# A transformer block pair on one Trainium2 core: the first attention loop one tile deeper

## What is computed

```
y = causal depthwise conv(x, 32 taps per sequence) + b
h = rmsnorm(y);  q = h q_w.T (16 heads of 128);  k, v = h k_w.T, h v_w.T (4 heads of 128)
q, k = rope(rmsnorm(q)), rope(rmsnorm(k))
hidden = y + softmax(causal(q k.T / sqrt(128))) v  @ o_w.T
x = x + hidden + moe(rmsnorm(hidden))           # 8 experts, top 2          -> layer 0
x = x + lora(adaLN transformer block(x, cond))  # attention, gelu FFN, top 1 of 8 -> layer 1
```

## Time and profile before

| | us |
|---|---|
| median of 3 runs | 723.17 |
| lowest, highest | 722.83, 726.57 |
| span of the profiled execution, first to last instruction | 724.2 |
| PE busy | 636.6 (88%) |
| DVE busy | 445.5 (62%) |
| ACT busy | 323.2 (45%) |
| POOL busy | 256.2 (35%) |

### The profile page before, as it was taken

One profiled execution on the slowest core, in us unless ns is written; L12 is line 12 of the kernel. 1 busy time (PEld: TensorE's weight loads), 2 busy tenths in 40 slices (PEclk: granted clock), 3 DMA queues, 4 the chain that ended last, 5 costly groups with the idle time before them and its releaser, 6 DMA issues.

```text
span 724.2 us, 12467 instructions
## 1 busy us (share of the span) xinstructions
PE 636.6 (88%) x4932; PEld 514.3 (71%) x4932; DVE 445.5 (62%) x804; ACT 323.2 (45%) x830; POOL 256.2 (35%) x257
## 2 busy tenths in 40 slices
PE   5379888889999688799995999999999998779997
PEld 2168657568777566688874888888888876558786
DVE  6999998767797766476548346236236235862363
ACT  5155455454567313343423555445444443346440
POOL 6619999914542403163214224014012003432100
PEclk9778999989999888899996999999999999879999
DMA  7500000000000005644510012001000002010013
GB/s 302 222 4 1 2 1 2 0 2 1 1 3 1 1 3 184 173 132 143 159 60 1 0 60 63 26 30 60 1 1 2 1 1 60 0 31 29 1 47 129
DMA packets 12361, 35.15 MB, mean 49 GB/s; under 512 B 2040, under 2 KB 3576, under 8 KB 11792
## 3 DMA queue, kind: packets, MB, share of 16 engines
q1 hardware_dynamic: 12304, 34.36, 14.3%
HBM read 33.24 MB, written 1.11 MB: 47 GB/s over the span
## 4 chain that ended last, share of the span: by engine, by line
PE 64%; POOL 14%; DVE 11%; ACT 5%; issue 3%; DMA 1%; SPq 0%; DVEq 0%; POOLq 0%; ACTq 0%
PE ps L1284 16%; PE ps L1285 15%; PE ps L1286 15%; PE ps L1377 5%; DVE yT L884 4%; POOL hid L479 4%; PE ps L1532 4%; POOL yT L481 3%; PE ps L1357 3%; POOL nrt L503 2%; PE ps L1683 2%; ACT work L645 1%; PE ps L1520 1%; ACT junk L580 1%; DVE strm_lo L1153 1%
## 5 line engine op out<-in xcount | busy, mean ns | idle before, releaser
L1153 DVE SCALAR_TENSOR_TENSOR strm_lo<-ps,col,strm_hi 128x512 fp32r<-128x512 f32 x32 | 24.0, 751 | 114.3 <-ACT strm_hi L763 113.2
L448 POOL TENSOR_TENSOR w_lo<-raw_w,w_hi 128x1024 fp32r<-128x1024 f32 x22 | 54.5, 2497 | 111.2 <-ACT w_hi L588 111.2
L1284 PE MATMUL ps<-act_hi,w_hi 128*128 128x512 f32 x160 | 65.4, 409 | 5.6 <-POOL act_lo L535 3.3
L747 ACT ACTIVATE work<-ps,col 128x512 f32<-128x512 f32 x64 | 44.2, 690 | 51.2 <-PE ps L1286 51.1
L1284 PE MATMUL ps<-w_hi,act_hi 128*128 128x512 f32 x160 | 65.1, 407 | 0.6 <-ACT junk L580 0.6
L1285 PE MATMUL ps<-act_lo,w_hi 128*128 128x512 f32 x160 | 64.1, 401 | 0.0
L1286 PE MATMUL ps<-act_hi,w_lo 128*128 128x512 f32 x160 | 64.1, 400 | 0.0
L1285 PE MATMUL ps<-w_lo,act_hi 128*128 128x512 f32 x160 | 63.9, 399 | 0.0
L1286 PE MATMUL ps<-w_hi,act_lo 128*128 128x512 f32 x160 | 63.5, 397 | 0.0
L1377 PE MATMUL ps<-raw_w,raw_s 128*128 128x256 f32 x256 | 58.8, 388 | 1.9 <-ACT raw_s L653 1.9
L1377 PEld LDWEIGHTS ps<-raw_w,raw_s 128*128 128x128 f32 x256 | 49.8, 195 | 12.7 <-issue 3.8
(11 more groups left out here) (179 smaller groups left out, 1569.7 us busy)
## 6 DMA issues: line engine op xcount, KB each, us to landing
raw_w<-in_w_attn SPq DMA_DIRECT2D x16, 512.0 KB, 4.7
raw_s<-in_w_moe SPq DMA_DIRECT2D x11, 384.0 KB, 4.4
raw_w<-in_w_qkv SPq DMA_DIRECT2D x6, 512.0 KB, 6.1
work<-comb_dram SPq DMA_DIRECT2D x10, 256.0 KB, 3.8
work<-comb_dram SPq DMA_DIRECT2D x18, 128.0 KB, 2.8
raw_w<-in_w_o SPq DMA_DIRECT2D x1, 2048.0 KB, 8.4
raw_s<-in_w_ffn SPq DMA_DIRECT2D x8, 256.0 KB, 2.7
bd<-in_w_ada SPq DMA_DIRECT2D x1, 1536.0 KB, 10.8
```

The lines of the kernel that those rows point to most:

```text
L448: G.tensor_tensor(flat(w_lo[:, slot]), raw_p[:, raw_slot, :], flat(f32(w_hi[:, slot])), ALU.subtract).then_inc(s_piece_lo, 1)
L747: A(dst[:, h * BANK:(h + 1) * BANK], src, ACT.Identity, bias=c_(b, 4 * j + h)).then_inc(s_q1_copied, 1)
L1153: V.scalar_tensor_tensor(flat(strm_lo[:, n % SS]), ps[:, 4 + n % 2, :], c_("bv", 4 * (u // CHUNKS) + h), flat(f32(strm_hi[:, n % SS])), AL ...
L1284: mm(dst, ah, bh, start=start and i == 0, stop=False, **flags)
```

## The change

The loops on TensorE, ScalarE and VectorE get a tenth step, and the back of the chain is one tile further behind. Step s is now: on TensorE the first two banks of `proj(s)`, `pv0(s-2)`, the other four banks, `oproj(s-2)`, `turn_qk(s)`, `scores0(s)`, `turn_y(s+1)`; on VectorE `rope(s)`, the head of softmax s-1, the addition of tile s-2, the tail of softmax s-1; on ScalarE the copies of two banks, the four copies of the value products of s-2, the other banks, three copies of qkT, exp of s-1, two copies of qkT, `take_y`. The factors, taps and DMAs keep their places on POOL and SP. The waits on bank 7 and the sums of squares of hid move by one step, and the transposes of hn of the first three tiles stand inside `oproj(7)` after four heads, those of the next three after twelve.

```diff
@@ -636,10 +636,10 @@
                 for h in range(4):
                     square(src[:, h * DH:(h + 1) * DH], DH, ssq[:, t % 2, at + h:at + h + 1])
 
-            def take_qkT(t):
+            def take_qkT(t, ks):
                 if t >= 1:
                     act.wait_ge(s_s0, t)
-                for k in range(QK):
+                for k in ks:
                     f = QK * t + k
                     act.wait_ge(s_qkT_in_psum, f + 1)
                     A(qkT[:, k * BANK:(k + 1) * BANK], ps[:, QK_BANK[k], :], ACT.Copy).then_inc(s_qkT_copied, 1)
@@ -654,28 +654,29 @@
 
             act.wait_ge(s_y1, DK)
             take_y(0)
-            for s in range(TILES + 1):
+            def exp0(t):
+                act.wait_ge(s_s0_shifted, t + 1)
+                A(sm_e[:], sm_s[:], ACT.Exp).then_inc(s_e0, 1)
+
+            for s in range(TILES + 2):
                 if s < TILES:
                     take_proj(s, 0)
-                if s >= 1:
-                    act.wait_ge(s_s0_shifted, s)
-                    A(sm_e[:], sm_s[:], ACT.Exp).then_inc(s_e0, 1)
+                    take_proj(s, 1)
+                if s >= 2:
+                    take_pv0(s - 2, range(HKV))
                 if s < TILES:
-                    for k in range(1, QK):
+                    for k in range(2, NPROJ):
                         take_proj(s, k)
-                if s >= 1:
-                    take_pv0(s - 1, (0, 1))
+                    take_qkT(s, range(3))
+                if 1 <= s <= TILES:
+                    exp0(s - 1)
                 if s < TILES:
-                    take_proj(s, QK)
-                if s >= 1:
-                    take_pv0(s - 1, (2, 3))
-                if s < TILES:
-                    take_qkT(s)
+                    take_qkT(s, range(3, QK))
                 if s < TILES - 1:
                     take_y(s + 1)
 
-                if s >= TILES - 1:
-                    for t in range(TILES - 1) if s == TILES - 1 else (TILES - 1,):
+                if s >= TILES:
+                    for t in range(TILES - 1) if s == TILES else (TILES - 1,):
                         act.wait_ge(s_hid_attn, t + 1)
                         square(hid[:, t, :], D, stat[:, 16 + t:17 + t])
             moe_slice_hi(0)
@@ -979,17 +980,23 @@
                 link(V.tensor_copy(act_hi[:, :, s], h2[:, :, s]))
                 V.tensor_tensor(act_lo[:, :, s], h2[:, :, s], f32(act_hi[:, :, s]), ALU.subtract).then_inc(s_h2_ready, 1)
 
-            for s in range(TILES + 1):
-                if s >= 1:
+            def add_attn(t):
+                dve.wait_ge(s_o0, t + 1)
+                dve.wait_ge(s_squares, (4 * QK + 1) * t + 1)
+                V.tensor_tensor(hid[:, t, :], ps[:, 7, 0:D], hid[:, t, :], ALU.add).then_inc(s_hid_attn, 1)
+
+            for s in range(TILES + 2):
+                if s < TILES:
+                    rope(s)
+                if 1 <= s <= TILES:
                     if s == 1:
                         dve.wait_ge(s_bd_zero, 1)
                     softmax0_head(s - 1)
+                    if 2 <= s < TILES:
+                        add_attn(s - 2)
+                    softmax_tail(s_e0, s, (s - 1) % 2, s_bd0, s_pv0, 4 * (s - 2) if s >= 3 else 0)
                     if s == TILES:
-                        for t in range(3):
-                            norm_h(t)
-                    softmax_tail(s_e0, s, (s - 1) % 2, s_bd0, s_pv0, 4 * (s - 2) if s >= 3 else 0)
-                if s < TILES:
-                    rope(s)
+                        add_attn(s - 2)
                 if s == 0:
 
                     dve.wait_ge(s_ada_mm, 1)
@@ -998,15 +1005,14 @@
                     dve.wait_ge(s_ada_ready, 1)
                     for i in (DK, 4 * DK):
                         link(V.tensor_scalar(ada[:, i:i + DK, :], ada[:, i:i + DK, :], 1.0, None, ALU.add))
-                if s == TILES:
+                if s == TILES + 1:
+                    for t in range(3):
+                        norm_h(t)
                     for t in range(TILES - 2):
                         to_h2(t)
                         if t + 3 < TILES - 1:
                             norm_h(t + 3)
-                if s >= 1:
-                    dve.wait_ge(s_o0, s)
-                    dve.wait_ge(s_squares, (4 * QK + 1) * (s - 1) + 1)
-                    V.tensor_tensor(hid[:, s - 1, :], ps[:, 7, 0:D], hid[:, s - 1, :], ALU.add).then_inc(s_hid_attn, 1)
+                    add_attn(TILES - 1)
                 if s < 3:
 
                     left = SEQ - TAPS0
@@ -1298,14 +1304,14 @@
             def turn_y(t):
 
                 pe.wait_ge(s_yw_ready, DK * (t // CT + 1))
-                if t >= 2:
-                    pe.wait_ge(s_hid_attn, t - 1)
+                if t >= 3:
+                    pe.wait_ge(s_hid_attn, t - 2)
                 for m in range(DK):
                     last = nc.tensor.transpose(ps[:, 7, m * P:(m + 1) * P], yT[:, m, tokens(t)], ident)
                 last.then_inc(s_ytok_T, 1)
 
-            def proj(t):
-                for k in range(NPROJ):
+            def proj(t, ks):
+                for k in ks:
                     if t == 0:
                         pe.wait_ge(s_piece_lo, k + 1)
                         if k == 2:
@@ -1359,15 +1365,18 @@
                        start=True, stop=True).then_inc(s_pv0, 1)
 
             def oproj(t):
-                if t + 1 < TILES:
-
-                    pe.wait_ge(s_ytok_copied, t + 2)
-                    pe.wait_ge(s_squares, (4 * QK + 1) * (t + 1) + 1)
+                if t + 2 < TILES:
+
+                    pe.wait_ge(s_ytok_copied, t + 3)
+                    pe.wait_ge(s_squares, (4 * QK + 1) * (t + 2) + 1)
                 else:
                     pe.wait_ge(s_hid_attn, t)
                 for h in range(HQ):
-                    if t == TILES - 1 and h == HQ // 2:
-
+                    if t == TILES - 1 and h == REP:
+                        pe.wait_ge(ld_small, 48)
+                        for i in range(3):
+                            turn_h(i)
+                    if t == TILES - 1 and h == 3 * REP:
                         for i in range(3, 6):
                             turn_h(i)
                         for i in range(3):
@@ -1395,9 +1404,15 @@
                 last.then_inc(s_glog, 1)
 
             turn_y(0)
-            for s in range(TILES + 1):
+            for s in range(TILES + 2):
                 if s < TILES:
-                    proj(s)
+                    proj(s, range(2))
+                if s >= 2:
+                    if s == 2:
+                        pe.wait_ge(ld_o0, 16)
+                    pv0(s - 2)
+                if s < TILES:
+                    proj(s, range(2, NPROJ))
                 if s == 0:
 
                     pe.wait_ge(ld_ada, 32)
@@ -1406,20 +1421,13 @@
                             last = mm(ps[:, 4, n * BATCH:(n + 1) * BATCH], wada[:, m, n * P:(n + 1) * P], cond[:, m, :],
                                       start=(m == 0), stop=(m == DK - 1))
                     last.then_inc(s_ada_mm, 1)
-                if s == TILES:
-                    pe.wait_ge(ld_small, 48)
-                    for t in range(3):
-                        turn_h(t)
-                if s >= 1:
-                    if s == 1:
-                        pe.wait_ge(ld_o0, 16)
-                    pv0(s - 1)
-                    oproj(s - 1)
+                if s >= 2:
+                    oproj(s - 2)
                 if s < TILES:
                     turn_qk(s)
-                    if s < TILES - 1:
-                        turn_y(s + 1)
                     scores0(s)
+                if s < TILES - 1:
+                    turn_y(s + 1)
 
             for t in range(3, 6):
                 logits0(t)
```

## The result

| | before | changed | predicted |
|---|---|---|---|
| median, us | 723.10 | 734.31 (733.35 to 736.31, 4 runs) | 735.8 (726.5 to 744) |
| ratio | 1 | 1.0153, 95% interval 1.0128 to 1.0179 | 1.0175 |
| span of the profiled execution | 724.2 | 732.3 | |

A forecast was written before the change was run, and what follows sets the result against it. It took POOL's taps to bound the loop until 148 us, then nearly equal TensorE and VectorE chains, then a drain. Terms 0.5 + 2.85 + 5.6 + 3.7 = +12.65 on the 723.17 us median gave 735.8 us, range 726.5 to 744.

The forecast's parts named there:

- before tile 4: Stretch up to the projection of tile 4, closed by POOL's taps: +0.5 us, taken between -1.4 and +1.7.
- tile 4: Tile 4 of the attention loop: 25.9 us plus 2.0 for the lower clock, against 25.05 before, +2.85 us.
- tiles 5 to 7, to the last scores: Loop up to the end of the last scores: 77.3 us against 71.70 before, +5.6 us.
- the end: Drain from last scores to last addition to hid: two tiles still owed, 26.5 us against 23.3, taken as +3.7.
- the rotation did wait for POOL in every tile: Sign on VectorE: its last rotation waits for POOL's norms in every tile.
- the bubble before the last value product: Sign in the drain: the 8.7 us between last scores and last value product before the change would be gone.
- the pause before the scores: Sign on TensorE: about 2.4 us of waiting before the scores, put down to ScalarE's copies of qkT, against 0.74.
- the end of the last scores: Sign at the loop's end: scores of the last tile near 255 us, against 247.11 before.
- the third rival: Loop: POOL is not late, a tile takes 24.5 us, the end +2.5; total 728.4 us, chance 0.17.
- The tile: One tile of the loop: 25.9 us against 23.72, through rotation of k, softmax head, exp, copies and scores.
- The low clock in every tile: First rival, TensorE in the loop: every tile starts at the lower clock, up to 1.9 us each; 741.4 us, chance 0.14.
- The faster rival: Loop: norms of k in time, TensorE's work sets a tile of 23.4 us; total 721.4 us, chance 0.09.

## Why the prediction was right, term by term

| term | predicted | in the traces |
|---|---|---|
| before tile 4 | +0.5 | 150.49 - 150.36 = +0.1 |
| tile 4 | +2.85 | (177.41 - 150.49) - 25.05 = +1.9 |
| tiles 5 to 7, to the last scores | +5.6 | (251.97 - 177.41) - 71.70 = +2.9 |
| the end | +3.7 | (281.26 - 251.97) - 23.33 = +6.0 |
| sum | +12.65 | +10.8 |

The sign and the sum held, and the end and the tiles were the places. The sizes did not: the tiles were put 3.7 us too high and the end 2.3 too low, and that the sum lies within 2 us of the forecast is in part luck. Of the signs named, the rotation did wait for POOL in every tile, and the bubble before the last value product is gone; the pause before the scores (1.47 for 2.4) and the end of the last scores (251.97 for 255) were missed. In the loop the third rival came nearest, with a tile of 24.5 us; its total, 728.4, failed at the end, for which it took 2.5 us.

*Before tile 4* the forecast had POOL's taps close the stretch. They did not: the last one ended at 147.60 + 0.24 = 147.84, and VectorE's split started at 148.82 behind its own softmax, with the norms of k 1.7 us later than before. That the scores of tile 3 no longer stood between took the delay back; the forecast had both terms, and left 0.5 of them.

*The tile* was put at 25.9 and took 24.78. Up to the rotation of k the chain ran 0.9 us shorter than worked out: the projection resumed at 6.8 (7.3), POOL began at 13.6 (13.9) and had the norms of k in 192.85 + 0.27 - 191.02 = 2.1 us, for which I had taken the 2.88 of rows 8, and the head ended at 21.6 (22.5). With that the head was no longer late for exp. The step that failed is therefore "scores s wait for exp s-1, that for the head of s-1, and that for the last rotation": the edges are in the code, but the last of them to bind was ScalarE's queue, five copies and exp in a row. The experiments agree: with the sums of squares earlier the wait stayed at 1.47, and at both other places of exp, with the value product still amid the projections, something behind it waited longer. With the value product behind the projections and exp early, nobody paid. Of the +1.06, exp is 0.5 and the open transpose 0.2; the rest, 0.36, is the value product, which takes 184.19 - 180.27 = 3.92 us instead of 3.66, and the restart behind it (0.4), less the gap of some 0.3 that stood before it.

*Tile 4* took 26.92 us, 2.1 over the tile of 24.78, where 2.0 had been put for the lower clock at its start; what was too high is the tile of 25.9 under it.

*The end* was too small by 2.3 us. I had the wait for the stream transposes (2.4 predicted, 2.44 measured) but let the value product behind it run at full clock; it took 5.46 us instead of 3.75. The other 0.6 lies within the 1.2 that I had left for VectorE's scaling of hid: TensorE waits 0.57 us for it at 277.21, and the last addition follows it on VectorE without a wait.

*The low clock in every tile,* the first rival, did not come: the pause was 1.47 us and not 2.4, and the scores behind it took 1.30. Where the pause was 2.38 and 2.70 us, before the scores of tiles 2 and 3, the scores took 1.81 and 1.85 instead of 1.30, so a pause of the forecast size can cost the clock. It need not: with the value product behind the projections the pause before the scores of tile 2 was 2.34 us, and they took 1.30. The rule on loops whose wait recurs, which the prediction took from the Trainium skill (TensorE: Matmul & The Clock Gate, section "HAM oscillation — how this bites in real kernels"), was thus not put to the test: no wait of 2.4 us recurred in every tile.

*The faster rival* had its place right: the value product amid the projections stalls. Put behind them, it gives 0.7%. A tile of 23.4 us was reached by no run.

## What to carry to other kernels

A software pipeline one step deeper takes no work off an engine that is already full. What it can win is the waits between steps, here 0.3 us a tile, and it owes a step at the end, here 10.6 us against a hole of 8.7. Before an instruction is moved on an in-order engine, read what stands behind it at the new place and who waits for that; a stall of 0.5 us here came back at each place of exp, until the value product moved as well. And where two engines end a step within 1 us of each other, as TensorE and VectorE do in rows 3 and 4, relieving one alone may gain nothing, as it did here for TensorE in the last tile (1.0000): the free time was in another stretch, where POOL was the end and VectorE stood still.

## What the runs showed of the hardware

POOL's small instructions ran faster where VectorE stood still: the factor on 128x4 took 0.34 us with VectorE idle for 2.15 us, against 0.77 while VectorE rotated. The Trainium skill, SBUF — State Buffer, section "Who interferes with whom", has VectorE's two-input operations in SBUF contend with GpSimd's reads. The trace agrees with that rule in sign, on this instruction in each of tiles 4 to 7 (0.77 to 0.78 before, 0.34 after), and it took 1.22 at 134.03 us of the changed kernel, where VectorE rotated; no run here separated the two engines for the purpose.

The first matmul of a projection that resumes behind the value product takes 0.64 us to the next one, and 0.31 where the projection follows the transpose of y. Why was not tried.
